# TensorE signals its groups through a drain instead of through the group's last matmul (two-layer kernel, one core)

## The chip, the cores and the metric

One core of one Trainium2 chip runs the kernel. The metric is device microseconds of one execution. TensorE runs matmuls and transpositions, VectorE (DVE), ScalarE (ACT) and GpSimd (POOL) do the element-wise work, SyncE (SP) issues most transfers. All five run their own instruction streams and meet only through semaphores that the kernel writes by hand.

## The reference, cut to what matters

Tokens are x [4, 1024, 128], float32. Two layers, each `x + mixer(norm(x)) + experts(norm(x))`:

```python
xn = layernorm(x)
x  = x + causal_attention(rope(xn @ wq.T), rope(xn @ wk.T), xn @ wv.T)  # scale 1/sqrt(128)
       + top1_experts(xn)         # 8 experts, capacity 512 tokens, one 128x128 matrix each
xn = layernorm(x)
h  = decay * (gelu(gelu(pos @ W1 + b1) @ W2 + b2) @ W3 + b3)            # a filter of 1024 x 128
x  = x + ((xn @ Wu + bu) * fftconv(xn @ Wv + bv, h)) @ Wo + bo
       + top2_experts(xn)         # 8 experts, 128 -> 256 -> relu -> 128
```

## The kernel before, in words

The work is cut into tiles of 128 tokens, 32 in all (`NT`). In order of time TensorE does the following. The order is written out by hand in `@block.tensor` from line 1070 on.

- **Start.** Two filter layers (`filter_layer`). For each of 4 sequences, `transpose_tokens` transposes 8 tiles in two groups of four, and `values_and_gates` multiplies them in four groups of two. Then `routing_counts(0)`.
- **Attention.** 32 rows of 128 queries. Step n of the loop issues `scores(n + 1)`, `transpose_probs(n)` (one or two groups), `weigh_values(n - 1)`. Between them stand `project` (queries and keys of the next sequence), `filter_layer(2)`, `filter_spectrum`, the eight experts of the first layer (`expert0_rows`, `expert0_out`) and `gates` of the second layer.
- **Middle.** `project_vu(0)` to `(3)`, `gates(3)`, `routing_counts(1)`, `project_vu(4)` to `(15)`. GpSimd then scatters 64 times rows to expert slots (line 758), in step with the transforms (`behind_transforms`).
- **Transforms.** `forward` 16 times and `inverse` 12 times, each one `dft` of four products of 128x256.
- **Experts.** The loop over 72 tiles (line 1366). Step n issues `expert_rows(n + 2)` (one transposition), `expert_hidden(n + 1)` (two products) and `expert_out(n)` (two products), plus the four last `inverse`, and `transpose_y` and `project_y` eight times each. ScalarE copies the weights of a tile's expert (line 1032) and the transposed rows (1039); ScalarE and VectorE take the hidden layer by turns (1046, 1748); VectorE adds the bias (1758); GpSimd sends the rows back (767).
- **Tail.** SyncE loads the returned rows, the other engines add them and the result is stored. TensorE has no work there.

All matmuls are issued by the helper `mm`, so the profile puts them on line 1077 whatever function they are from. A float32 product is two MATMUL instructions and two LDWEIGHTS; a transposition is one of each. A group is what stands between two signals. In the kernel before, the group's last instruction carries the signal:

```python
                for f in range(2):
                    last = mm(S[0][:, n % 2, f * P:(f + 1) * P], w12r[:, n % W_RING, f * P:(f + 1) * P], xsT[:, n % 2, :])
                last.then_inc(e_h, 1)
```

Of the kernel before, what the change touches and what calls it, by code (L numbers as in the profile page):

```python
# [26 lines left out]
P = 128  # L27
D = 128
# [3 lines left out]
J = L // P  # L32
# [190 lines left out]
def two_layer_kernel(nc, x_in, cst_in, rope_in, fw_in, iv_in, pe_in, wqk_in, wvg_in, w0_in, b0_in,  # L223
# [3 lines left out]
    with ctx:  # L227
# [847 lines left out]
        def _(pe):  # L1075
# [15 lines left out]
            def values_and_gates(g):  # L1091
                for u in range(4):
                    n = 4 * g + u
                    pe.wait_ge(tr_free, 2 * g + u // 2 + 1)
                    if n >= 2:
                        pe.wait_ge(vg_free, n - 1)
                    for q in range(2):
                        i = 2 * n + q
                        last = mm(O[n % 2][:, q * VGW:(q + 1) * VGW], xT[:, i * P:(i + 1) * P], wvg)
                    last.then_inc(vg_full, 1)  # L1100

            def routing_counts(k):

                pe.wait_ge(rt, (R0_OH, R1_OH)[k])
                if k:
                    pe.wait_ge(lg1_done, B)
                    pe.wait_ge(o_done, NT)
                oh = ohb[:, :, :].rearrange("p e i -> p (e i)")
                mm(O[0][:, 0:E * NT], beforeb[:, :], oh)
                mm(O[0][:, E * NT:2 * E * NT], onesb[:, :], oh).then_inc(rt_mm, 1)  # L1110

            def filter_layer(k):

                if k:
                    pe.wait_ge(f_pool, 4 * k)
                if k < 2:
                    for h in range(2):
                        r = (pe_sb[0:FO, :], hg[0:FO, :])[k][:, 512 * h:512 * h + 512]
                        last = mm(S[k][0:FO, h, :], (f1w, f2w)[k], r)
                else:  # L1120
                    pe.wait_ge(twos_done, 1)
                    for j in range(J):
                        if j % 4 == 0:
                            wait_emptied(pe, T_USES, T_AT[("h", j // 4)])
                        last = mm(t_bank("h", j // 4)[:, (j % 4) * P:(j % 4) * P + P], hg[0:FO + 1, j * P:(j + 1) * P], f3w)
                last.then_inc(f_full, 1)
# [17 lines left out]
            def project(b, h):  # L1144

                for u in (2 * h, 2 * h + 1):
                    n = 4 * b + u
                    slot = S[(n + 1) % 2]
                    wait_scores_bank(("pr", n))
                    for a in range(2):  # L1150
                        last = mm(slot[:, a, :], wqk[:, 2 * (u % 2) + a, :],
                                  xT[:, b * L + 512 * (u // 2):b * L + 512 * (u // 2) + 512])
                    last.then_inc(pr_full, 1)

            def scores(n):
                b, i = n // J, n % J
                wait_scores_bank(("s", n))
                pe.wait_ge(rope_done, 4 * b + (2 if i < 4 else 4))
                q = qk[b % 2][:, 0, i * P:(i + 1) * P]
                for c in range((i + 4) // 4):  # L1160
                    w = min(512, (i + 1) * P - 512 * c)
                    diagonal = c == i // 4
                    last = mm(S[n % 2][:, c, 0:w], q, qk[b % 2][:, 1, 512 * c:512 * c + w], stop=not diagonal)
                    if diagonal:
                        last = mm(S[n % 2][:, c, w - P:w], identb[:, :], maskb[:, :], start=False)
                last.then_inc(s_full, 1)

            def wait_scores_bank(use):

# [5 lines left out]
            def transpose_probs(n):  # L1175
                i = n % J
                pe.wait_ge(exp_done, n + 1)
                for c in range((i + 4) // 4):
                    wait_emptied(pe, T_USES, T_AT[("p", n, c)])
                    for j in range(4 * c, min(4 * c + 4, i + 1)):  # L1180
                        last = pe.transpose(t_bank("p", n, c)[:, (j - 4 * c) * P:(j - 4 * c + 1) * P],  # L1181
                                            prob[n % 2][:, j * P:(j + 1) * P], ident)
                    last.then_inc(pt_full, 1)

            def weigh_values(n):
                b, i = n // J, n % J
                wait_emptied(pe, O_USES, O_AT[("o", n)])
                pe.wait_ge(pt_act, n + 1)
                for j in range(i + 1):
                    if j == 4:  # L1190
                        pe.wait_ge(pt_dve, SECOND.index(n) + 1)
                    last = mm(o_bank("o", n)[:, 0:D], pT[n % 2][:, j, :], vsb[:, b * J + j, :], start=j == 0, stop=j == i)
                last.then_inc(o_full, 1)

            def gates(g):

                for u in (2 * g, 2 * g + 1):
                    wait_emptied(pe, T_USES, T_AT[("t", u)])
                    for q in range(4):
                        pe.wait_ge(xn_done, NT + 4 * u + q + 1)  # L1200
                        last = pe.transpose(t_bank("t", u)[:, q * P:(q + 1) * P], row[:, 4 * u + q, 0:D], ident)
                    last.then_inc(tr_full, 1)
                pe.wait_ge(l1_w_loaded, 16 * N_L1W)
                wait_emptied(pe, O_USES, O_AT[("g", g)])
                for i in range(J * g, J * g + J):
                    pe.wait_ge(tr_free, 2 * B + i // 4 + 1)
                    last = mm(o_bank("g", g)[:, (i % J) * E:(i % J) * E + E], xT[:, i * P:(i + 1) * P], wg1[:, :])
                last.then_inc(g_full, 1)

            def expert0_rows(e):  # L1210
                wait_emptied(pe, T_USES, T_AT[("x", e)])
                for t in range(GROUP):
                    k = GROUP * e + t
                    pe.wait_ge(xs_loaded[k % RING[0]], turn(0, k))
                    last = pe.transpose(t_bank("x", e)[:, t * P:(t + 1) * P], row_slots[0][k % RING[0]][:, 0:D], ident)
                last.then_inc(e_t[0], 1)

            def expert0_out(e):
                pe.wait_ge(moe0_w_loaded, 32)
                pe.wait_ge(e_xT[0], e + 1)  # L1220
                wait_emptied(pe, O_USES, O_AT[("y", e)])
                for t in range(GROUP):
                    last = mm(o_bank("y", e)[:, t * D:(t + 1) * D], xsT0[e % 2][:, t * P:(t + 1) * P], w0[:, e, :])
                last.then_inc(e_y[0], 1)

            pe.wait_ge(filt_loaded, 32)
            filter_layer(0)
# [37 lines left out]
            def project_vu(u):  # L1265
# [4 lines left out]
                for t in range(4):  # L1270
                    i = 4 * (u % 8) + t
                    mm(o[:, t * D:(t + 1) * D], pickb[0:96, :], biasb[0:96, (BV_AT, BU_AT)[u // 8]:(BV_AT, BU_AT)[u // 8] + D],
                       stop=False)
                    last = mm(o[:, t * D:(t + 1) * D], xT[:, i * P:(i + 1) * P], (wv, wu)[u // 8][:, :], start=False)
                last.then_inc(uvg_full, 1)

            pe.wait_ge(exp_done, NT)
            pe.wait_ge(split_done, len(PARTS))
# [41 lines left out]
            def transpose_y(q):  # L1320
# [3 lines left out]
                wait_c_emptied(pe, "yt", q)  # L1324
                for t in range(4):
                    b, j = divmod(4 * q + t, J)
                    last = pe.transpose(c_bank("yt", q)[:, t * P:(t + 1) * P],
                                        vv[b // 2][:, j, (b % 2) * D:(b % 2 + 1) * D], ident)
                last.then_inc(yt_full, 1)

            def project_y(q):
                pe.wait_ge(yt_free, q + 1)
                wait_c_emptied(pe, "wo", q)
                for t in range(4):
                    i = 4 * q + t
                    o = c_bank("wo", q)[:, t * D:(t + 1) * D]
                    mm(o, pickb[0:96, :], biasb[0:96, BO_AT:BO_AT + D], stop=False)
                    last = mm(o, yT[:, i * P:(i + 1) * P], wo[:, :], start=False)
                last.then_inc(wo_full, 1)

            def expert_rows(n):
                pe.wait_ge(xs_loaded[n % RING[1]], turn(1, n))
                if n >= 2:
                    pe.wait_ge(e_xT[1], n - 1)
                pe.transpose(TP[n % 2][:, 0:P], row_slots[1][n % RING[1]][:, 0:D], ident).then_inc(e_t[1], 1)  # L1346

            def expert_hidden(n):
                pe.wait_ge(e_xT[1], n + 1)
# [1 line left out]
                if n >= 2:  # L1351
                    wait_hidden(pe, n - 2)
                for f in range(2):
                    last = mm(S[0][:, n % 2, f * P:(f + 1) * P], w12r[:, n % W_RING, f * P:(f + 1) * P], xsT[:, n % 2, :])
                last.then_inc(e_h, 1)

            def expert_out(n):
                we = w12r[:, n % W_RING, H1 + 2:W_COLS]
# [470 lines left out]
```

## Time and profile before

| | |
|---|---|
| median of 3 runs | 549.97 us (547.23 to 551.78) |
| the profiled execution's own time | 549.17 us |
| its span, first to last instruction | 547.0 us |
| mean granted TensorE clock in the span | 0.864 |
| TensorE busy with matmuls | 385.5 us |
| VectorE, GpSimd, ScalarE busy | 305.4, 284.3, 201.0 us |

In the rows below PE is TensorE's matmuls, PEld its weight loads, and an engine with a q (PEldq) its sequencer. Lines are start, length, engine, line, operation and tiles; the number behind x is a count. In brackets is the time that the engine had stood idle ahead of the instruction and what released it. The ends of matmuls are modelled. A granted clock of 1.00 is 2.4 GHz, 0.50 is 1.2 GHz.

### The profile page before, as it was taken

Reading aid. Unit: us, or ns where it says so; the run is one execution under the profiler, and the core shown is the slowest. Engines: PE = TensorE matmul, PEld = TensorE weight load, DVE = VectorE, ACT = ScalarE, POOL = GpSimd, SP = SyncE. Lnnn points to the kernel's source line nnn. Section 1 sums busy time; section 2 is a strip of 40 time slices with the busy share of each in tenths; the row PEclk is TensorE's granted clock in tenths of the full one; section 3 lists DMA queues with packets and bytes.
Section 4 is the critical chain, followed back from the end, with each engine's and each line's share of the span. In section 5 each row is a group of like instructions: output and inputs, shape, how many; then the busy total and the mean of one; then the engine's idle time right before and its main releaser. Section 6 shows DMA issues by size and latency. Waiting matters only on the chain.

```text
span 547.0 us, 8125 instructions
## 1 busy us (share of the span) xinstructions
PE 385.5 (70%) x2228; PEld 307.3 (56%) x2228; DVE 305.4 (56%) x807; ACT 201.0 (37%) x501; POOL 284.3 (52%) x283
## 2 busy tenths in 40 slices
PE   2573858869696977987785975934977898778600
PEld 0451425756574655686784753823856887667600
DVE  4968428513672675634989961401456576755364
ACT  1471222233241336532230001122766565656360
POOL 2836465425455577401197775762455555555443
PEclk9998787989798999888699695985999799989955
DMA  9999931723211111100001231313122222221094
GB/s 251 402 224 232 178 70 36 198 71 83 60 53 40 58 40 40 38 1 1 5 11 44 71 104 60 104 48 80 43 79 74 70 64 65 74 76 55 11 324 137
DMA packets 63305, 50.27 MB, mean 92 GB/s; under 512 B 7314, under 2 KB 58200, under 8 KB 63006
## 3 DMA queue, kind: packets, MB, share of 16 engines
q1 hardware_dynamic: 56704, 36.92, 27.1%
q0 software_dynamic: 6400, 12.50, 7.2%
q10 hardware_dynamic: 158, 0.33, 0.3%
q8 instruction: 19, 0.31, 0.2%
q14 instruction: 24, 0.20, 0.1%
HBM read 26.18 MB, written 24.22 MB: 92 GB/s over the span
## 4 chain that ended last, share of the span: by engine, by line
PE 24%; POOL 11%; issue 11%; DVE 6%; ACT 3%; DMA 2%; another core or an unknown queue 2%; ACTq 1%; DVEq 1%; POOLq 0%; SPq 0%
PE psS L1077 12%; POOL slots L758 11%; PE psO L1077 9%; PE psT L1346 1%; DVE xres L1780 1%; DMA work<-moe 1%; ACTq L1029 1%; ACT row L958 1%; ACT xsT L1039 1%; DVEq L1754 1%; DVE hT L1748 1%; ACT work L941 0%; DMA slots<-row,slot 0%; ACT xT L964 0%
## 5 line engine op out<-in xcount | busy, mean ns | idle before, releaser
L758 POOL DMA_INDIRECT slots<-row,slot x96 | 109.1, 1136 | 76.1 <-issue 29.0
L767 POOL DMA_INDIRECT moe<-ys,xs x64 | 63.7, 996 | 74.8 <-DVE ys L1758 37.5
L1077 PE MATMUL psS<-work 128*128 128x512 f32 (+3 forms) x96 | 44.0, 574 | 23.2 <-DVE work L1557 13.9
L1077 PE MATMUL psS<-xsT,w12r 128*128 128x128 f32 x288 | 51.5, 306 | 11.7 <-ACT xsT L1039 11.5
L1032 ACT ACTIVATE w12r<-w 128x514 f32 x72 | 45.6, 633 | 30.9 <-PE psO L1077 22.1
L1077 PE MATMUL psO<-w12r,hT 128*128 128x128 f32 x288 | 49.5, 297 | 10.0 <-issue 7.2
L1077 PEld LDWEIGHTS psS<-xsT,w12r 128*128 128x128 f32 x288 | 41.3, 207 | 18.2 <-ACT xsT L1039 15.6
L1077 PEld LDWEIGHTS psO<-w12r,hT 128*128 128x128 f32 x288 | 40.8, 204 | 13.8 <-issue 12.7
L951 ACT ACTIVATE work<-psT 128x512 f32<-128x512 f32 (+3 forms) x32 | 16.5, 515 | 85.2 <-PE psT L1181 72.2
L1077 PE MATMUL psO<-work 128*128 128x128 f32 x288 | 41.6, 294 | 5.3 <-DVE xres L1582 5.3
L1758 DVE TENSOR_TENSOR ys<-psO,b 128x128 f32<-128x128 f32 x72 | 20.8, 289 | 40.8 <-PE psO L1077 29.0
L1748 DVE TENSOR_SCALAR hT<-psS,w12r 128x128 f32<-128x128 f32 x72 | 21.8, 344 | 37.6 <-PE psS L1077 37.0
L1077 PEld LDWEIGHTS psO<-work 128*128 128x128 f32 x288 | 38.6, 210 | 5.5 <-DVE xres L1582 5.5
L1077 PEld LDWEIGHTS psS<-work 128*128 128x128 f32 x96 | 18.7, 224 | 39.8 <-issue 20.4
L1582 DVE SCALAR_TENSOR_TENSOR xres<-psO,work,xres 128x128 f32<-128x128 f32 x32 | 11.1, 348 | 46.3 <-PE psO L1077 28.1
L1077 PE MATMUL psS<-xT,work 128*128 128x512 f32 x64 | 32.5, 649 | 4.5 <-ACT work L941 4.4
L1564 DVE TENSOR_REDUCE work<-psS 128x1 f32<-128x128 f32 (+7 forms) x32 | 24.1, 753 | 20.6 <-PE psS L1077 17.7
L767 POOL DMA_INDIRECT moe<-ys,w x24 | 23.4, 975 | 18.4 <-DVE ys L1758 11.7
L941 ACT ACTIVATE work<-psS,work 128x128 f32<-128x128 f32 (+7 forms) x32 | 23.6, 738 | 17.7 <-DVE work L1568 17.1
L1077 PE MATMUL psS<-xT,mats 128*128 128x256 f32 x96 | 25.6, 410 | 2.3 <-issue 2.2
L1181 PE MATMUL psT<-cst,work 128*128 128x128 f32 x144 | 23.3, 293 | 4.8 <-ACT work L941 4.7
L1017 ACT ACTIVATE work<-psT 128x512 f32<-128x512 f32 x4 | 2.4, 597 | 63.3 <-remote 54.5
(285 smaller groups left out, 863.7 us busy)
## 6 DMA issues: line engine op xcount, KB each, us to landing
slots<-xs SPq DMA_DIRECT2D x13, 516.0 KB, 14.9
xs<-slots SPq DMA_DIRECT2D x64, 64.5 KB
work<-moe SPq DMA_DIRECT2D x8, 512.0 KB, 3.9
xres<-in_x SPq DMA_DIRECT2D x4, 512.0 KB, 9.2
mats<-in_fw SPq DMA_DIRECT2D x1, 2048.0 KB, 11.4
moe<-xs SPq DMA_DIRECT2D x4, 512.0 KB, 7.9
mats<-in_iv SPq DMA_DIRECT2D x8, 256.0 KB
xT<-moe SPq DMA_DIRECT2D x4, 512.0 KB, 8.2
```

The lines of the kernel that those rows point to most:

```text
L758: pool.indirect_dma_start(dst[:, :], bass.IndirectOffsetOnAxis(ap=slots[:, i:i + 1], axis=0), row[:, i, :], None, bounds_check=bound, oob_ ...
L767: pool.indirect_dma_start(dst[:, :], bass.IndirectOffsetOnAxis(ap=row_slots[l][m][:, D:ROWW].bitcast(I32), axis=0), ys[:, n % UNROLL, :], ...
L941: act.activation(prob[n % 2][:, 0:(i + 1) * P], S[n % 2][:, :, :].rearrange("p a m -> p (a m)")[:, 0:(i + 1) * P], ACT.Exp, bias=negmax[:, ...
L951: act.activation(pT[n % 2][:, 0:k, :].rearrange("p j q -> p (j q)"), t_bank("p", n, 0)[:, 0:k * P], ACT.Copy).then_inc(pt_act, 1)
L958: act.activation(row[:, i, 0:D], xres[:, i, :], ACT.Identity, bias=nbias[:, i:i + 1], scale=rstd[:, i:i + 1]).then_inc(xn_done, 1)
L1032: act.activation(w12r[:, n % W_RING, :], w12[:, bass.ds(e, 1), :].rearrange("p e h -> p (e h)"), ACT.Copy).then_inc(e_w1, 1)
L1077: return pe.matmul(o, lhsT, rhs, start=start, stop=stop)
L1181: last = pe.transpose(t_bank("p", n, c)[:, (j - 4 * c) * P:(j - 4 * c + 1) * P], prob[n % 2][:, j * P:(j + 1) * P], ident)
L1564: dve.tensor_reduce(negmax[:, n:n + 1], S[n % 2][:, :, :].rearrange("p a m -> p (a m)")[:, 0:(n % J + 1) * P], X, ALU.max, negate=True).th ...
L1582: stt(xres[:, n, :], o_bank("o", n)[:, 0:D], rrec[:, n:n + 1], xres[:, n, :], ALU.mult, ALU.add).then_inc(o_done, 1)
L1748: last = ts(hT[:, n % 2, f, :], S[0][:, n % 2, f * P:(f + 1) * P], w12r[:, n % W_RING, H1 + f:H1 + f + 1], 0.0, ALU.add, ALU.max)
L1758: tt(ys[:, m, :], O[n % 2][:, 0:D], b2[:, bass.ds(e, 1), :].rearrange("p e d -> p (e d)"), ALU.add).then_inc(e_ys[1], 1)
```

## The change

In every function of `@block.tensor` that signals, the increment no longer rides on the last matmul or transposition of the group. A `pe.drain()` is issued behind it and carries the increment. Matmuls, transpositions, weight loads, waits and the order of the groups stay as they are. In the diff, cut to the forms that it takes:

```diff
@@ transpose_tokens
-                        last = pe.transpose(TP[u][:, q * P:(q + 1) * P], row[:, i, 0:D], ident)
-                    last.then_inc(tr_full, 1)
+                        pe.transpose(TP[u][:, q * P:(q + 1) * P], row[:, i, 0:D], ident)
+                    pe.drain().then_inc(tr_full, 1)
@@ routing_counts
-                mm(O[0][:, E * NT:2 * E * NT], onesb[:, :], oh).then_inc(rt_mm, 1)
+                mm(O[0][:, E * NT:2 * E * NT], onesb[:, :], oh)
+                pe.drain().then_inc(rt_mm, 1)
@@ dft
-                    last = mm(o[n], mats[:, c, 2 * n + 1, :], a[:, 1, :], start=False)
-                last.then_inc(s, 1) if s else None
+                    mm(o[n], mats[:, c, 2 * n + 1, :], a[:, 1, :], start=False)
+                pe.drain().then_inc(s, 1) if s else None
@@ expert_rows
-                pe.transpose(TP[n % 2][:, 0:P], row_slots[1][n % RING[1]][:, 0:D], ident).then_inc(e_t[1], 1)
+                pe.transpose(TP[n % 2][:, 0:P], row_slots[1][n % RING[1]][:, 0:D], ident)
+                pe.drain().then_inc(e_t[1], 1)
@@ expert_out
-                mm(O[n % 2][:, 0:D], hT[:, n % 2, 1, :], we[:, D:2 * D], start=False).then_inc(e_y[1], 1)
+                mm(O[n % 2][:, 0:D], hT[:, n % 2, 1, :], we[:, D:2 * D], start=False)
+                pe.drain().then_inc(e_y[1], 1)
...
```

The same is done in `values_and_gates`, `filter_layer`, `project`, `scores`, `transpose_probs`, `weigh_values`, `gates`, `expert0_rows`, `expert0_out`, `project_vu`, `transpose_y`, `project_y` and `expert_hidden`.

## Rows read from the trace of the kernel before

**Rows 1.** The page, busy time and instructions of each engine.
```profile
PE 385.5 (70%) x2228; PEld 307.3 (56%) x2228; DVE 305.4 (56%) x807; ACT 201.0 (37%) x501; POOL 284.3 (52%) x283
```
**Rows 2.** Busy time in six stretches: start, attention, middle, transforms, experts, tail.
```profile
core 0: us, PE busy (x) PEld busy (x) DVE busy (x) ACT busy (x) POOL busy (x), PEclk, DMA share, GB/s
0.00:53.70 53.70, 25.71 (x114) 16.78 (x114) 39.36 (x123) 20.40 (x51) 28.33 (x25) 0.97 1.09 279
53.70:248.10 194.40, 157.41 (x868) 114.63 (x869) 97.64 (x287) 66.76 (x157) 94.79 (x105) 0.88 0.30 69
248.10:283.80 35.70, 27.36 (x216) 25.64 (x215) 28.23 (x68) 11.29 (x21) 14.16 (x5) 0.85 0.01 3
283.80:376.90 93.10, 59.77 (x224) 47.30 (x224) 44.02 (x86) 7.69 (x13) 64.42 (x65) 0.79 0.23 69
376.90:515.00 138.10, 115.25 (x808) 102.90 (x808) 80.40 (x213) 84.69 (x227) 68.82 (x70) 0.93 0.24 66
515.00:547.00 32.00, 0.00 (x0) 0.00 (x0) 15.73 (x31) 10.20 (x32) 13.79 (x15) 0.55 0.62 197
```
**Rows 3.** TensorE's waits among the experts, 376.9 to 515: total, times, longest.
```profile
PE psS L1077 <- ACT xsT L1039: 11.5, 13, 1.6
PE psO L1077 <- issue: 7.2, 6, 1.9
PE psO L1077 <- DVE hT L1748: 2.5, 5, 0.8
PE psS L1077 <- DVE xres L1741: 1.2, 2, 0.7
```
**Rows 4.** The block's end (line 227), TensorE's sequencer: duration min/median/max.
```profile
L227 PEldq DRAIN  x1: 712/712/712, 514.3 to 514.3; - x1
```
**Rows 5.** Timeline of the last products of TensorE.
```profile
514.29 0.68 PE L1077 MATMUL psO<-w12r,hT 128*128 128x128 f32 x4 [0.21 <-DVE hT L1748]
```
**Rows 6.** One tile each at clock 0.50 and 1.00, TensorE back to back.
```profile
425.58 1.06 PE L1077 MATMUL psS<-xsT,w12r 128*128 128x128 f32 x4
426.44 1.06 PE L1077 MATMUL psO<-w12r,hT 128*128 128x128 f32 x4
427.29 0.42 PE L1346 MATMUL psT<-cst,xs 128*128 128x128 f32 x1
427.50 1.06 PE L1077 MATMUL psS<-xsT,w12r 128*128 128x128 f32 x4
...
429.42 0.61 PE L1077 MATMUL psS<-xsT,w12r 128*128 128x128 f32 x4
429.87 0.61 PE L1077 MATMUL psO<-w12r,hT 128*128 128x128 f32 x4
430.32 0.27 PE L1346 MATMUL psT<-cst,xs 128*128 128x128 f32 x1
430.43 0.68 PE L1077 MATMUL psS<-xsT,w12r 128*128 128x128 f32 x4
```
**Rows 7.** One hidden-layer instruction, 404 to 412 and then 425 to 429: min/median/max ns.
```profile
L1077 PE MATMUL psS<-xsT,w12r x22: 275/275/377, 404.0 to 412.0; 128*128 128x128 f32 x22
```
```profile
L1077 PE MATMUL psS<-xsT,w12r x8: 421/421/421, 425.6 to 428.1; 128*128 128x128 f32 x8
```
**Rows 8.** Waits of TensorE's sequencer in `expert_hidden` (line 1345).
```profile
L1345 PEldq EVENT_SEMAPHORE  x70: 51/51/51, 377.8 to 509.9; - x70
```
**Rows 9.** Timeline of a restart of TensorE behind ScalarE.
```profile
407.05 0.62 ACT L1046 ACTIVATE hT<-psS,w12r 128x128 f32<-128x128 f32 x2 [0.59 <-PE psS L1077]
407.79 0.52 PEld L1077 LDWEIGHTS psO<-w12r,hT 128*128 128x128 f32 x4 [0.75 <-issue]
407.82 0.68 PE L1077 MATMUL psO<-w12r,hT 128*128 128x128 f32 x4 [0.59 <-issue]
```
**Rows 10.** Timeline of TensorE ahead of and in a stretch at clock 0.50 (422.6 to 429.4).
```profile
421.86 0.68 PE L1077 MATMUL psO<-w12r,hT 128*128 128x128 f32 x4 [1.92 <-issue]
422.38 0.27 PE L1346 MATMUL psT<-cst,xs 128*128 128x128 f32 x1
423.50 1.22 PE L1077 MATMUL psS<-xsT,w12r 128*128 128x128 f32 x4 [0.85 <-ACT xsT L1039]
```
**Rows 11.** TensorE's waits in the attention, 53.7 to 248.1.
```profile
PE psS L1077 <- DVE work L1557: 13.9, 5, 5.2
...
PE psO L1077 <- DVE xres L1582: 5.3, 1, 5.3
...
PE psT L1215 <- DMA xs<-slots: 4.0, 1, 4.0
```
**Rows 12.** Timeline where the transforms start and end, and at the first expert tile.
```profile
283.82 2.40 PE L1077 MATMUL psS<-work,mats 128*128 128x256 f32 x10 [1.50 <-DVE work L635]
```
```profile
359.77 1.97 PE L1077 MATMUL psO<-xT,mats 128*128 128x256 f32 x8 [0.89 <-issue]
376.94 0.88 PE L1346 MATMUL psT<-cst,xs 128*128 128x128 f32 x2 [15.20 <-DMA xs<-slots]
```
**Rows 13.** The program's start (line 1820), TensorE's sequencer.
```profile
L1820 PEldq DRAIN  x1: 8/8/8, 0.3 to 0.3; - x1
```

More of the change, by code:

```diff
@@ L1098, in values_and_gates @@
                         i = 2 * n + q
-                        last = mm(O[n % 2][:, q * VGW:(q + 1) * VGW], xT[:, i * P:(i + 1) * P], wvg)
-                    last.then_inc(vg_full, 1)
+                        mm(O[n % 2][:, q * VGW:(q + 1) * VGW], xT[:, i * P:(i + 1) * P], wvg)
+                    pe.drain().then_inc(vg_full, 1)
             def routing_counts(k):
@@ L1118, in filter_layer @@
                         r = (pe_sb[0:FO, :], hg[0:FO, :])[k][:, 512 * h:512 * h + 512]
-                        last = mm(S[k][0:FO, h, :], (f1w, f2w)[k], r)
+                        mm(S[k][0:FO, h, :], (f1w, f2w)[k], r)
                 else:
@@ L1124, in filter_layer @@
                             wait_emptied(pe, T_USES, T_AT[("h", j // 4)])
-                        last = mm(t_bank("h", j // 4)[:, (j % 4) * P:(j % 4) * P + P], hg[0:FO + 1, j * P:(j + 1) * P], f3w)
-                last.then_inc(f_full, 1)
+                        mm(t_bank("h", j // 4)[:, (j % 4) * P:(j % 4) * P + P], hg[0:FO + 1, j * P:(j + 1) * P], f3w)
+                pe.drain().then_inc(f_full, 1)
             def dft(o, a, c, s):
@@ L1150, in project @@
                     for a in range(2):
-                        last = mm(slot[:, a, :], wqk[:, 2 * (u % 2) + a, :],
+                        mm(slot[:, a, :], wqk[:, 2 * (u % 2) + a, :],
                                   xT[:, b * L + 512 * (u // 2):b * L + 512 * (u // 2) + 512])
-                    last.then_inc(pr_full, 1)
+                    pe.drain().then_inc(pr_full, 1)
             def scores(n):
@@ L1162, in scores @@
                     diagonal = c == i // 4
-                    last = mm(S[n % 2][:, c, 0:w], q, qk[b % 2][:, 1, 512 * c:512 * c + w], stop=not diagonal)
+                    mm(S[n % 2][:, c, 0:w], q, qk[b % 2][:, 1, 512 * c:512 * c + w], stop=not diagonal)
                     if diagonal:
-                        last = mm(S[n % 2][:, c, w - P:w], identb[:, :], maskb[:, :], start=False)
-                last.then_inc(s_full, 1)
+                        mm(S[n % 2][:, c, w - P:w], identb[:, :], maskb[:, :], start=False)
+                pe.drain().then_inc(s_full, 1)
             def wait_scores_bank(use):
@@ L1180, in transpose_probs @@
                     for j in range(4 * c, min(4 * c + 4, i + 1)):
-                        last = pe.transpose(t_bank("p", n, c)[:, (j - 4 * c) * P:(j - 4 * c + 1) * P],
+                        pe.transpose(t_bank("p", n, c)[:, (j - 4 * c) * P:(j - 4 * c + 1) * P],
                                             prob[n % 2][:, j * P:(j + 1) * P], ident)
-                    last.then_inc(pt_full, 1)
+                    pe.drain().then_inc(pt_full, 1)
             def weigh_values(n):
@@ L1191, in weigh_values @@
                         pe.wait_ge(pt_dve, SECOND.index(n) + 1)
-                    last = mm(o_bank("o", n)[:, 0:D], pT[n % 2][:, j, :], vsb[:, b * J + j, :], start=j == 0, stop=j == i)
-                last.then_inc(o_full, 1)
+                    mm(o_bank("o", n)[:, 0:D], pT[n % 2][:, j, :], vsb[:, b * J + j, :], start=j == 0, stop=j == i)
+                pe.drain().then_inc(o_full, 1)
             def gates(g):
@@ L1200, in gates @@
                         pe.wait_ge(xn_done, NT + 4 * u + q + 1)
-                        last = pe.transpose(t_bank("t", u)[:, q * P:(q + 1) * P], row[:, 4 * u + q, 0:D], ident)
-                    last.then_inc(tr_full, 1)
+                        pe.transpose(t_bank("t", u)[:, q * P:(q + 1) * P], row[:, 4 * u + q, 0:D], ident)
+                    pe.drain().then_inc(tr_full, 1)
                 pe.wait_ge(l1_w_loaded, 16 * N_L1W)
@@ L1206, in gates @@
                     pe.wait_ge(tr_free, 2 * B + i // 4 + 1)
-                    last = mm(o_bank("g", g)[:, (i % J) * E:(i % J) * E + E], xT[:, i * P:(i + 1) * P], wg1[:, :])
-                last.then_inc(g_full, 1)
+                    mm(o_bank("g", g)[:, (i % J) * E:(i % J) * E + E], xT[:, i * P:(i + 1) * P], wg1[:, :])
+                pe.drain().then_inc(g_full, 1)
             def expert0_rows(e):
@@ L1214, in expert0_rows @@
                     pe.wait_ge(xs_loaded[k % RING[0]], turn(0, k))
-                    last = pe.transpose(t_bank("x", e)[:, t * P:(t + 1) * P], row_slots[0][k % RING[0]][:, 0:D], ident)
-                last.then_inc(e_t[0], 1)
+                    pe.transpose(t_bank("x", e)[:, t * P:(t + 1) * P], row_slots[0][k % RING[0]][:, 0:D], ident)
+                pe.drain().then_inc(e_t[0], 1)
             def expert0_out(e):
@@ L1222, in expert0_out @@
                 for t in range(GROUP):
-                    last = mm(o_bank("y", e)[:, t * D:(t + 1) * D], xsT0[e % 2][:, t * P:(t + 1) * P], w0[:, e, :])
-                last.then_inc(e_y[0], 1)
+                    mm(o_bank("y", e)[:, t * D:(t + 1) * D], xsT0[e % 2][:, t * P:(t + 1) * P], w0[:, e, :])
+                pe.drain().then_inc(e_y[0], 1)
             pe.wait_ge(filt_loaded, 32)
@@ L1273, in project_vu @@
                        stop=False)
-                    last = mm(o[:, t * D:(t + 1) * D], xT[:, i * P:(i + 1) * P], (wv, wu)[u // 8][:, :], start=False)
-                last.then_inc(uvg_full, 1)
+                    mm(o[:, t * D:(t + 1) * D], xT[:, i * P:(i + 1) * P], (wv, wu)[u // 8][:, :], start=False)
+                pe.drain().then_inc(uvg_full, 1)
             pe.wait_ge(exp_done, NT)
@@ L1326, in transpose_y @@
                     b, j = divmod(4 * q + t, J)
-                    last = pe.transpose(c_bank("yt", q)[:, t * P:(t + 1) * P],
+                    pe.transpose(c_bank("yt", q)[:, t * P:(t + 1) * P],
                                         vv[b // 2][:, j, (b % 2) * D:(b % 2 + 1) * D], ident)
-                last.then_inc(yt_full, 1)
+                pe.drain().then_inc(yt_full, 1)
             def project_y(q):
@@ L1337, in project_y @@
                     mm(o, pickb[0:96, :], biasb[0:96, BO_AT:BO_AT + D], stop=False)
-                    last = mm(o, yT[:, i * P:(i + 1) * P], wo[:, :], start=False)
-                last.then_inc(wo_full, 1)
+                    mm(o, yT[:, i * P:(i + 1) * P], wo[:, :], start=False)
+                pe.drain().then_inc(wo_full, 1)
             def expert_rows(n):
@@ L1353, in expert_hidden @@
                 for f in range(2):
-                    last = mm(S[0][:, n % 2, f * P:(f + 1) * P], w12r[:, n % W_RING, f * P:(f + 1) * P], xsT[:, n % 2, :])
-                last.then_inc(e_h, 1)
+                    mm(S[0][:, n % 2, f * P:(f + 1) * P], w12r[:, n % W_RING, f * P:(f + 1) * P], xsT[:, n % 2, :])
+                pe.drain().then_inc(e_h, 1)
             def expert_out(n):
```

## The prediction

> **What bounds the kernel now.** I read the page's busy times first. TensorE leads with 385.5 of 547.0 us [rows 1]. That average hides stages with different limits, so I cut the span into six stretches [rows 2]. Among the experts TensorE is busy 115.3 of 138.1 us, in the attention 157.4 of 194.4, and no other engine reaches 62% of either stretch. Its waits among the experts sum to 22.4 us in 26 pieces, none over 1.9 us [rows 3]. Those two stages, 332 of 547 us, are TensorE's. The other four are not, or only partly. The start is shared with loads and VectorE. In the middle TensorE leads into the routing and VectorE finishes it. The transforms are set by GpSimd: TensorE's last inverse transform starts at 359.8, and its next instruction waits 15.2 us for rows that GpSimd scatters [rows 12]. The tail has no TensorE work.
>
> **How many drains.** One per signal, from the loops.
> - Start: 2 filter layers + 8 transposition groups + 16 value groups + 1 routing = 27.
> - Attention: 16 projections + 32 scores + 48 transposition groups + 32 value products + 1 filter layer + 4 spectra + 8 + 8 experts + 9 in the first three `gates` = 158.
> - Middle: 16 + 3 + 1 = 20.
> - Transforms: 16 forward + 12 inverse = 28.
> - Experts: 3 x 72 + 4 inverse + 8 + 8 = 236.
>
> The sum is 469. No matmul is added or taken away.
>
> **What one drain does.** The old program has a drain on TensorE at its end. It begins at 514.3 and takes 712 ns, so it ends near 515.02 [rows 4]. The four products that it covers start at 514.29 and end at 514.97 [rows 5]. It was issued with three of the four still to start, held its sequencer until all were complete, and ended 0.05 us later. That 0.05 us is what a drain adds to a signal that another engine is waiting for. A start rounded to 0.1 us leaves 0.00 to 0.09.
>
> The larger part is what it takes from TensorE. Now the next group follows the last product at the pace of the stream. One tile takes 430.43 - 429.42 = 1.01 us for nine instructions, 0.11 each [rows 6]. One instruction by itself takes 0.275 from start to end [rows 7]. With a drain the next group can't be issued until the last has ended. From the last start to the next I count four steps:
> - 0.275 to the end of the last product;
> - 0.05 for the drain;
> - 0.05 for the EVENT_SEMAPHORE that most groups have for their further waits [rows 8];
> - 0.06 for LDWEIGHTS and the start of the matmul. ScalarE ends at 407.67 and the matmul starts at 407.82, 0.15 later. Of that 0.05 is the EVENT_SEMAPHORE and about 0.04 the way of the signal [rows 9].
>
> That is 0.435 in place of 0.11, so 0.32 lost. A group that starts on an empty engine takes 0.68 instead of 0.61 [rows 6, 9], 0.07 more. One drain at a place where TensorE ran on therefore costs 0.39 us at clock 1.00. At clock 0.50 the instruction takes 0.421 [rows 7], the pace is (427.50 - 425.58) / 9 = 0.213 [rows 6], and a group after a wait takes 1.22 in place of 1.06 [rows 6, 10]. There a drain costs 0.421 + 0.16 - 0.213 + 0.16 = 0.53. The lowest bound is a drain that adds no gap beyond completion, 0.275 - 0.11 = 0.165. The highest is 0.53 everywhere. I take 0.39 because it is built from restarts that this trace has.
>
> **Experts.** Of 236 places 26 have a wait already [rows 3], and no gap is added there. 210 x 0.39 = 82 us. The new gaps give ScalarE and VectorE time to answer, so the 22.4 us of waits can vanish: 82 - 22 = 60. Without that it is 82. With more overlap than I see, 48.
>
> Then the clock. It was 0.50 from 422.6 to 429.4, just behind waits of 1.92 and 0.85 us, and rose behind a run of tiles back to back [rows 6, 10]. A regular tile now holds 1.01 us of streaming. With three gaps it takes 1.01 + 3 x 0.39 = 2.18, and no regular stretch is back to back any more. So I expect more falls, and fewer of the runs behind which the clock rose. A tile at 0.50 takes 1.92 + 3 x 0.53 = 3.51 us, 1.33 more. I take a third of the tiles, 24 x 1.33 = 32 us, less some 6 that the present low stretches cost already: +26. With two thirds it is 48 x 1.33 - 6 = +58. The dense projections and inverse transforms lie between and should lift it again. Experts: 60 + 26 = 86 us, from 48 to 118.
>
> The Trainium skill (TensorE: Matmul & The Clock Gate, "A second HAM failure mode: psum-queue depth-cycling") describes a kernel whose frequent small idles between groups made the gate swing between its two levels. The trace agrees as far as its falls stand behind waits; it holds no stretch with small gaps alone.
>
> **Attention.** 158 places, some 21 with a wait already: 137 x 0.39 = 53.4. Waits on something not itself behind TensorE can swallow gaps: 5.3 for VectorE's `xres`, 4.0 for a load, and a few of the 13.9 for VectorE's rotations [rows 11]. I take 12. The rotations start with a TensorE signal, so most of that wait stays. Later signals at the waits add 21 x 0.05 = 1, and a few more low stretches 4 (the clock is 0.88 there already [rows 2]). 46 us, from 30 to 62 + 8.
>
> **Start.** 27 places at 0.39 are 10.5. Part of it lies beside loads and VectorE's 39 busy microseconds [rows 2]. 7 us, from 3 to 10.
>
> **Middle and transforms.** `project_vu(0)` to `(3)` and `gates(3)` lead into the routing: 7 x 0.39 = 2.7. The twelve later `project_vu` add 4.7 beside VectorE, while the first transform has 1.5 us of idle ahead of it [rows 12], so 3.2 shows there. Behind it GpSimd's scatters set the pace, with 15.2 us of TensorE idle at the end as cover for the 28 drains (28 x 0.39 = 11). If that cover were gone, all 48 would cost 19. I take 6, from 3 to 15.
>
> **Tail.** Nothing.
>
> **Sum.** 7 + 46 + 6 + 86 = 145 us. The profiled execution took 549.2 (span 547.0 and 2.2 around it), which is 0.8 below the median of the runs, nothing here. 549.2 + 145 = 694.
>
> **Rivals.**
> - *The clock stays up.* The gaps are short, and today's falls stand behind gaps over 0.8 us. Against it: three gaps in each tile take over half of its time. Then 7 + 42 + 6 + 60 = 115, so 664.
> - *The clock stays down among the experts.* If once fallen it finds nothing dense to rise behind, two thirds of the tiles run at 0.50. Experts 118, attention 50, middle and transforms 8, start 7: 183, so 732. Against it: the first tiles and each sequence's projections are dense.
> - *A drain costs only the pipeline's tail.* With 0.165 + 0.05 = 0.21 at some 390 places it is 82, less 34 swallowed: 48 us and 597. Against it: restarts here take longer. The Trainium skill (TensorE: Matmul & The Clock Gate, "Single matmul latency") puts the constant part of a lone product at 398 cycles of 2.4 GHz, 166 ns; by its price alone 469 drains would be an estimated 78 us and the time 627. The 0.165 of rows 6 and 7 agrees with it.
> - *Not slower: the drain doesn't hold what is behind it.* If TensorE's queue takes the next weights and matmuls past a drain, only sequencer time is added, hidden because the sequencer runs ahead, and 0.05 us at some 50 waits: 552. It decides for this if the start-to-start distance across a drain stays near 0.11. For it: the first drain takes 8 ns [rows 13]. Against it: TensorE was empty then; the one with work ahead took 712. By the Trainium skill (PSUM — Partial Sum Buffer, "Engine vs sequencer instructions") a drain waits until the engine is fully idle, which would rule this rival out; the 712 ns agree.
>
> **How the numbers follow.** Forecast 0.42 (694), clock up 0.28 (664), clock down 0.20 (732), tail only 0.07 (597), not slower 0.03 (552). The low end is 3 + 30 + 3 + 48 = 84, so 633. The high end is 10 + 62 + 15 + 118 = 205, so 754. With 0.10 below and some 0.07 above, the range 633 to 755 holds about eight in ten. A change of about 1% can be told from none. Faster by over 1%: 0.01, for the chance that shifted transfers collide less. Within 1%: 0.02. Slower: 0.97.
>
> **What would show it.** 469 more DRAIN rows on TensorE's sequencer, ending about 0.05 us behind the last product. TensorE's matmul count unchanged. Start-to-start across a group's border 0.4 to 0.5 us in place of 0.11. The experts' stretch 220 to 230 us long with a mean clock near 0.8, the attention's near 240, the tail unchanged at 32. The forecast is wrong if the distance stays under 0.3 (the third rival), if the clock among the experts is over 0.93 (the first) or near 0.6 (the second), or if a large part of the added time stands among the transforms, where I give GpSimd the lead.

## The result and the profile after

The changed kernel takes 766.6 us, the median of 4 runs (757.3 to 784.0), and the kernel before 548.6 (546.8 to 551.8). The forecast was 694 us with a range of 633 to 755, so the direction was right and the size was not. The profiled execution took 770.3 us for a span of 768.2 at a mean granted clock of 0.717. The runs of the changed kernel differ by more than is usual (757.3 us at a mean clock of 0.740, 784.0 at 0.701), and the ratio of 1.385, with a 95% interval of 1.370 to 1.400, takes only the two shorter ones, 757.3 and 762.8, as the later ratios leave out the slower executions too and so are not the quotients of the medians beside them.

The page of the changed kernel, busy times, answers to [rows 1]. The second line is the granted clock over 40 slices of the span, in tenths.

```profile
PE 576.0 (75%) x2228; PEld 396.1 (52%) x2228; DVE 310.5 (40%) x807; ACT 208.2 (27%) x501; POOL 285.0 (37%) x283
...
PEclk9997789869979997755899867555555555555555
```

TensorE has the same 2228 matmuls and is "busy" 190 us longer. No other engine gained more than 7.2 us. The trace has 8594 instructions in place of 8125, one more for each of the 469 drains. From slice 26 on the clock is 5 without a break. The six stretches of [rows 2], cut at the same places of the program within 1 us:

```profile
0.00:72.20 72.20, 43.02 (x114) 24.75 (x115) 39.38 (x123) 20.84 (x51) 28.38 (x25) 0.97 1.06 244
72.20:307.20 235.00, 191.64 (x865) 119.69 (x866) 99.24 (x286) 66.91 (x157) 94.25 (x105) 0.87 0.16 46
307.20:362.80 55.60, 43.00 (x219) 35.45 (x219) 28.41 (x69) 11.40 (x21) 27.85 (x19) 0.59 0.06 18
362.80:444.00 81.20, 59.22 (x224) 42.56 (x225) 43.97 (x86) 7.80 (x13) 51.15 (x51) 0.90 0.23 68
444.00:736.80 292.80, 239.09 (x808) 173.69 (x808) 83.79 (x213) 91.09 (x227) 70.26 (x71) 0.53 0.11 31
736.80:768.20 31.40, 0.00 (x0) 0.00 (x0) 15.75 (x31) 10.21 (x32) 13.08 (x14) 0.50 0.63 201
```

| stretch | before | forecast | after | added |
|---|---|---|---|---|
| start | 53.7 | +7 | 72.2 | +18.5 |
| attention | 194.4 | +46 | 235.0 | +40.6 |
| middle and transforms | 128.8 | +6 | 136.8 | +8.0 |
| experts | 138.1 | +86 | 292.8 | +154.7 |
| tail | 32.0 | 0 | 31.4 | -0.6 |

The 0.97 in the start's row is no reading of the clock there. The matmuls of that stretch have the lengths of half clock, as two rows further down show.

The drains among the experts, behind the hidden layer, and a tile of the changed kernel:

```profile
L1357 PEldq DRAIN  x72: 685/1195/1200, 445.3 to 732.7; - x72
```
```profile
561.39 0.45 PE L1347 MATMUL psT<-cst,w 128*128 128x128 f32 x1 [0.23 <-issue]
...
562.06 1.20 PE L1077 MATMUL psS<-xsT,w12r 128*128 128x128 f32 x4 [0.23 <-ACT w12r L1032]
...
563.49 1.19 PE L1077 MATMUL psO<-w12r,hT 128*128 128x128 f32 x4 [0.23 <-issue]
...
564.91 0.45 PE L1347 MATMUL psT<-cst,w 128*128 128x128 f32 x1 [0.23 <-issue]
```

The drain holds the sequencer for the length of its group, here 1.19 us. Behind 226 of the 236 groups of the stretch TensorE stands idle for some 0.23 us, although nothing that the next group needs is late. The tile takes 564.91 - 561.39 = 3.52 us, and 3.51 was forecast for a tile at clock 0.50. TensorE's waits of [rows 3] have gone into these pieces of 0.23:

```profile
PE psO L1077 <- issue: 16.5, 70, 0.3
PE psT L1347 <- issue: 16.3, 70, 0.3
PE psS L1077 <- ACT w12r L1032: 12.1, 52, 0.3
```

### The profile page after: what moved, and what is told of

The parts are those of the page before. It is cut to its first block, busy times and chain, and to the rows that moved or that the text cites. A ratio compares the mean times of both kernels' runs of the same rounds, so it can differ in the third digit from the quotient of the medians.

```text
span 768.2 us, 8594 instructions
## 1 busy us (share of the span) xinstructions
PE 576.0 (75%) x2228; PEld 396.1 (52%) x2228; DVE 310.5 (40%) x807; ACT 208.2 (27%) x501; POOL 285.0 (37%) x283
## 4 chain that ended last, share of the span: by engine, by line
PEld 22%; issue 16%; PEldq 13%; DVE 6%; ACT 5%; DMA 2%; ACTq 0%; POOL 0%; SPq 0%; DVEq 0%; POOLq 0%
PEld psS L1077 14%; PEldq L1366 7%; PEld psO L1077 6%; ACT w12r L1032 4%; PEldq L1357 2%; DVE ys L1711 1%; DVE xres L1783 1%; PEldq L567 1%; DMA work<-moe 1%; PEldq L1134 1%; PEldq L1348 1%; PEld psS L1328 1%; PEld psT L1347 0%; DVE late L1711 0%; DVE hT L1711 0%
## 5 line engine op out<-in xcount | busy, mean ns | idle before, releaser
L1077 PE MATMUL psS<-xsT,w12r 128*128 128x128 f32 x288 | 83.7, 444 | 16.9 <-ACT w12r L1032 12.1
L1077 PE MATMUL psO<-w12r,hT 128*128 128x128 f32 x288 | 83.7, 445 | 16.7 <-issue 16.5
L1077 PEld LDWEIGHTS psS<-xsT,w12r 128*128 128x128 f32 x288 | 65.0, 314 | 35.4 <-issue 34.2
L1077 PEld LDWEIGHTS psO<-w12r,hT 128*128 128x128 f32 x288 | 65.0, 314 | 35.4 <-issue 35.4
L1077 PE MATMUL psO<-work 128*128 128x128 f32 x288 | 45.5, 310 | 10.2 <-issue 8.6
L1077 PE MATMUL psS<-xT,work 128*128 128x512 f32 x64 | 41.0, 775 | 5.0 <-issue 2.8
L1347 PE MATMUL psT<-cst,xs 128*128 128x128 f32 x48 | 20.8, 433 | 20.9 <-issue 10.7
L1182 PE MATMUL psT<-cst,work 128*128 128x128 f32 x144 | 27.9, 307 | 8.9 <-issue 6.6
L1046 ACT ACTIVATE hT<-psS,w12r 128x128 f32<-128x128 f32 x72 | 22.5, 363 | 37.6 <-PEq L1357 37.6
L1077 PE MATMUL psS<-biasb,pickb 96*128 96x128 bf16 x96 | 27.9, 291 | 3.3 <-issue 2.1
```

Of the source, the lines that this page charges most:

```text
L1046: last = act.activation(hT[:, n % 2, f, :], S[0][:, n % 2, f * P:(f + 1) * P], ACT.Relu, bias=w12r[:, n % W_RING, H1 + f:H1 + f + 1])
L1077: return pe.matmul(o, lhsT, rhs, start=start, stop=stop)
```

## The experiments

Most kernels of this section are made with one helper in the place of the 469 drains, and a variable `stage` that names the stretch:

```diff
+            def signal(s):
+                if stage[0] in ("experts",):      # or the stretches that an experiment names
+                    pe.drain().then_inc(s, 1)
+                else:
+                    last[0].then_inc(s, 1)        # the group's last matmul or transposition
-                pe.drain().then_inc(e_h, 1)
+                signal(e_h)
```

**Where the time is: drains by stretch.** The helper as above; the second run has the other four stretches instead.

> Drains only among the experts (236 of 469), elsewhere the signal rides on the last instruction as before. Theory A (the gaps behind the drains thin the stream so that the granted clock falls and does not come back in this stretch): the experts' stretch is 294 us as in the changed kernel, against 138 before, its clock about 0.53, the other stretches as before: 549 + 156 = 705 us. Rival B (the low clock there was chance or was brought along from the stages ahead): the clock among the experts is over 0.85 and the stretch some 200 us, in all about 610 us.

> Drains everywhere but among the experts (233 of 469). Theory A: start +19, attention +41, middle +19, transforms -13 as the two profiles stand against each other, experts 138 us at a clock near 0.93: 549 + 66 = 615 us. Rival B (low clock brought along): the experts' stretch is well over 138 us with a clock under 0.8 though it has no drain.

With drains among the experts alone it took 694.8 us (690.6 to 697.3) where the kernel before took 550.3 on the same chip: +144.5. The other way round it took 614.6 (608.4 to 617.6): +64.3. Together that is 209 of the 218 us by which the medians differ. The experts' stretch of the first, then of the second:

```profile
371.70:657.50 285.80, 232.20 (x808) 168.45 (x808) 83.73 (x213) 90.72 (x227) 70.42 (x71) 0.55 0.11 32
```
```profile
439.60:574.30 134.70, 111.17 (x808) 100.32 (x808) 80.21 (x213) 83.90 (x227) 69.19 (x70) 0.96 0.24 67
```

The low clock comes with the drains of this stretch and isn't brought along: behind stages full of drains, tiles without them run at 0.96. That is theory A.

**Late signal or late start.** All 469 drains stay, but the signal goes back to the last instruction ahead of them. Then, a second drain behind each.

```diff
             def signal(s):
+                last[0].then_inc(s, 1)
-                pe.drain().then_inc(s, 1)
+                pe.drain()
```

> All 469 drains stay, but the signal rides on the last instruction of the group again, ahead of the drain. Theory A (the cost is that TensorE starts its next group late): within 12 us of the changed kernel, 750 to 770 us. Rival D (the cost is that the other engines hear later): most of the added 218 us goes away, 550 to 620 us.

> A second drain behind each of the 469. Theory A: TensorE is empty when it comes, so it costs some 0.05 us of sequencer time, 469 x 0.05 = 23 us: 780 to 795 us. Rival F (a drain has a price of its own of the size of a restart, 0.3 us or more): over 880 us.

The first took 755.9 us (754.5 to 758.4). The other engines hear at once again, and the added time is still there: 205.6 of 218 us by the medians, and all of it by the ratios, 1.388 against 1.385. It is TensorE's own late start that costs. Even what is left is mostly not the earlier signal. The experts' stretch of this trace is 276.2 us where the changed kernel's is 292.8. A tile takes 3.48 us in place of 3.52, which is 3 us in all. The rest comes from the clock, which fell later: between the first inverse transforms and its fall there are 13 plain tiles of some 2.32 us here, and one in the trace of the changed kernel. The second took 806.2 (804.9 and 807.4, two runs only), 40 more than the median with one drain, where 13 to 28 were expected. A row of it shows the piece of idle at 0.30 where it was 0.23:

```profile
605.98 1.19 PE L1080 MATMUL psS<-xsT,w12r 128*128 128x128 f32 x4 [0.30 <-issue]
```

So a drain on an empty engine costs 0.07 us by this row, and 0.08 by the spans of the two profiles (805.3 - 768.2 = 37 us for 469), somewhat more than the 0.05 I gave it, and far from a restart. Rival F falls.

**The two small stretches.** The helper with "start" and with "middle" alone.

> Drains only in the start, 27 of 469. Theory A: in the changed kernel the clock first rose at 64.4 us and not at 26.6, so the start is 18 us longer: first score product at 72 us where it was 54, in all 567 us. Rival H (27 drains at the price of clock 1.00, 0.39 us, no more): 10.5 us, first score product by 64 us, 560 us or less.

> Drains only in the middle, 20 of 469. Theory A: the projections fall to clock 0.50 and stay there, the middle takes 55 us in place of 36; GpSimd starts its scatters at the same time as before, so the transforms give about 10 back: 556 to 562 us. Rival I (VectorE and GpSimd hide all of it): middle at most 42 us and 549 to 552 us in all.

Start alone: 563.7 us (560.6 to 570.1) where the kernel before took 545.9, ratio 1.036 (1.024 to 1.049). The first score product stands at 72.1, as in the changed kernel. 27 drains cost 18 us, 0.67 each, more than the 0.53 of clock 0.50. The rest is the clock, as the value groups show. First the kernel before, two groups in one line, then two late groups of the changed kernel:

```profile
27.63 1.19 PE L1077 MATMUL psO<-work,xT 128*128 128x136 f32 x8 [0.25 <-ACT xT L870]
```
```profile
51.28 1.24 PE L1077 MATMUL psO<-work,xT 128*128 128x136 f32 x4 [0.23 <-issue]
52.75 1.25 PE L1077 MATMUL psO<-work,xT 128*128 128x136 f32 x4 [0.23 <-issue]
```

Eight instructions took 1.19 us, now four take 1.24. Before, these groups ran at full clock from 27 us on. In the changed kernel the last of them, at 52.75, is still at half clock, and so are those of the kernel with drains in the start alone.

Middle alone: 553.6 us (548.8 to 555.7) where the kernel before took 545.9, ratio 1.022 (1.009 to 1.034). That is 8 us by the medians and 12 by the ratio, within the 7 to 13 of theory A (556 to 562 less 549) and over the 0 to 3 of rival I, though the profiled execution, the shortest of its runs, shows only 2 us more in these two stretches. The middle and the transforms of it:

```profile
243.70:297.60 53.90, 42.69 (x221) 35.09 (x218) 28.62 (x69) 11.39 (x21) 26.74 (x18) 0.60 0.05 16
297.60:374.80 77.20, 54.46 (x225) 44.77 (x225) 43.80 (x86) 7.69 (x13) 52.26 (x52) 0.88 0.24 73
```

The middle runs at 0.60 and takes 18 us more than before, and the transforms give 16 of it back. GpSimd's first and last scatter of this run:

```profile
268.06 1.12 POOL L758 DMA_INDIRECT slots<-row,slot  x1 [20.55 <-DVE slot L1709]
...
370.49 0.97 POOL L758 DMA_INDIRECT slots<-row,slot  x1 [0.30 <-issue]
```

They lie 102.4 us apart. In the kernel before it was 101.8 (270.81 to 372.59), in the one with all drains 107.7 (331.86 to 439.55). GpSimd's chain sets the end of the transforms, and the drains of the middle hardly reach it: that is the cover that the forecast gave. The cover isn't whole for the drains of the transforms. Where they are there the chain is 6 us longer, also in the kernel with drains everywhere but among the experts (107.8). In the trace of the changed kernel GpSimd waits 13.5 us in 9 pieces for drains of `dft`.

**One, two, three drains per tile.** The helper asks for the semaphore instead of the stretch.

```diff
-                if stage[0] in ("experts",):
+                if any(s is d for d in (e_h,)):                   # one per tile
+                if any(s is d for d in (e_h, e_y[1])):            # two
+                if any(s is d for d in (e_t[1], e_h, e_y[1])):    # three
```

> Of the drains only the 72 behind the hidden-layer products of the expert tiles. Theory A (the clock stays up while the stream is thick enough, so the cost is not in proportion to the drains): 72 x 0.39 = 28 us less what the 22 us of waits take in, clock among the experts over 0.85: 555 to 575 us. Rival E (each drain costs its share of what all 236 cost there, 145 us): 145 x 72 / 236 = 44, so 594 us.

> Of the drains only the 144 behind the two groups of products of the expert tiles, none behind their transpositions. A tile at clock 1.00 is then 1.01 + 2 x 0.39 = 1.79 us, at 0.50 1.92 + 2 x 0.53 = 2.98. Theory A: the stream is between that of one and of three drains; the clock falls for part of the stretch, 0.7 to 0.95, stretch 172 to 215 us, in all 585 to 625 us. Rival E (in proportion): 145 x 144 / 236 = 88, so 638 us.

> Drains behind all three groups of the 72 expert tiles (216) and nowhere else, so none on the 20 inverse transforms, transpositions and projections of the same stretch. Theory A (the third drain of a tile is what takes the clock): clock under 0.7 among the experts, 670 to 695 us. Rival L (the 20 others are what takes it, by thinning the only dense work there): clock over 0.85 and 590 to 610 us, in line with 568 for one drain per tile and 577 for two.

| drains among the experts | us | before beside it | added | per drain | clock there | stretch |
|---|---|---|---|---|---|---|
| 72 | 567.5 (564.5 to 573.6) | 551.0 | 16.6 | 0.23 | 0.91 | 156.0 |
| 144 | 576.7 (574.9 to 579.7) | 551.0 | 25.8 | 0.18 | 0.97 | 164.4 |
| 216 | 682.9 (681.7 to 689.0) | 548.3 | 134.6 | 0.62 | 0.56 | 272.7 |
| 236 | 694.8 (690.6 to 697.3) | 550.3 | 144.5 | 0.61 | 0.55 | 285.8 |

The stretch of 144 drains, then of 216, then one tile of the first:

```profile
379.70:544.10 164.40, 132.47 (x808) 106.20 (x808) 82.61 (x213) 87.07 (x227) 70.27 (x70) 0.97 0.19 55
```
```profile
375.80:648.50 272.70, 223.56 (x808) 165.12 (x808) 83.73 (x213) 90.72 (x227) 70.36 (x71) 0.56 0.12 33
```
```profile
481.65 0.68 PE L1080 MATMUL psO<-w12r,hT 128*128 128x128 f32 x4 [0.23 <-issue]
...
483.60 0.68 PE L1080 MATMUL psO<-w12r,hT 128*128 128x128 f32 x4 [0.23 <-issue]
```

The first 144 drains are cheap: the waits that were there take in a part of each, and the clock stays up. With 144 it is 0.97, where the kernel before has 0.93. A tile takes 483.60 - 481.65 = 1.95 us. The 1.01 of [rows 6] holds only where nothing waited: from 391.1 to 440.2 the kernel before took 49.0 us for 28 tiles, 1.75 each. The 72 behind one transposition each bring 109 us with them, 1.5 us per drain, and take the clock. The 20 on the denser groups are 10 us. Rival L falls, and so does any account in proportion. Whether it is the number of gaps in a tile that takes the clock, or the transposition that now stands alone between two of them, isn't tested: no run has two drains of which one is behind the transposition. For two drains my own expectation (585 to 625) was too high, because I looked for falls of the clock that did not come.

**More work, less time.** One bf16 product of 256 or 384 columns ahead of each of the 216 groups, into columns of the group's own bank that nobody reads. No other engine waits for it.

```diff
+            def filler(o):
+                for r in range(1):                 # 2 in the second of these kernels
+                    mm(o, onesb[0:96, :], biasb[0:96, 0:o.shape[1]])
 ...
+                filler(TP[n % 2][:, P:P + 384])
                 transpose(TP[n % 2][:, 0:P], row_slots[1][n % RING[1]][:, 0:D], ident)
```

> As the kernel with drains only among the experts, and ahead of each of the 216 groups of the tiles one more bf16 product of 256 or 384 columns into unused columns of the group's own bank; its result is used by nobody. Theory A: the stream is thicker, the clock there goes to over 0.85, a tile takes about 2.7 us in place of 3.52 although it has more to do: stretch about 225 us, in all about 636 us, 70 us less than without the filler. Rival C (a drain lowers the clock itself, or the clock has nothing to do with how thin the stream is): the clock stays at 0.5, a tile takes about 4.4 us, in all about 770 us.

> Drains only among the experts, and two fillers ahead of each group instead of one. Theory A: the clock was up with one already, so the second only adds its stream, 0.11 to 0.16 us each at 2.4 GHz: 216 x 0.14 = 30 us, 660 us. Rival K (more stream still gains clock): 630 us or less.

> The changed kernel with all 469 drains and the fillers ahead of the 216 groups of the expert tiles. Theory A: the experts come down from 294 to about 220 us as they did with drains there alone, the other stretches stay: 766 - 70 = 696 us, between 685 and 705. Rival J (with low clock brought along from the stages ahead the fillers don't lift it): 760 us or more.

With drains among the experts alone, one filler per group brings 694.8 us down to 630.3 (626.9 to 634.3). The fillers add 216 matmuls and take 64 us away. The expert stretch:

```profile
377.60:597.80 220.20, 166.10 (x1024) 117.37 (x1022) 83.63 (x213) 90.51 (x227) 70.09 (x70) 0.98 0.15 41
```

The clock is 0.98 in place of 0.55, with every drain still there. So a drain doesn't lower the clock by itself. With two fillers the clock is 0.98 too, the stretch is 252.0 and the run 664.5 (659.2 to 665.2). That is 34 more, the stream of the second filler and nothing gained. In the kernel with all 469 drains one filler gives 699.7 us (692.9 to 703.7), 67 less than the 766.6 of the changed kernel, with 220.6 us for the stretch, the other stretches as they were.

So the drains have two costs, and the clock is the larger. The 64 us that the fillers gave back are less than the clock costs, for the fillers need time themselves. At clock 1.00 a tile with three drains takes 2.35 us (rows in the next section), with one filler per group 2.61 (420.05 to 422.66 in that trace). So one set of fillers is an estimated 72 x 0.26 = 19 us, and the stretch with all its drains, at full clock and without fillers, an estimated 220 - 19 = 201 us. That is 63 over the 138 of the kernel before, for the gaps. The other 92, up to the 293 of the changed kernel, are the clock. The tiles alone say nearly the same: 72 x (3.52 - 2.35) = 84 us. The fillers differ from the other matmuls in more than being additional (bf16, 256 or 384 columns), and which of that brings the clock back isn't shown.

**The same on the kernel before.** No drain; useless products only where TensorE waited anyway.

```diff
             project(0, 0)
+            for _ in range(8):
+                mm(TP[0][:, :], ident, cst[:, 0:512])
 ...
             pe.wait_ge(b_free, INV_BEFORE)
+            for _ in range(12):
+                mm(TP[0][:, :], ident, cst[:, 0:512])
```

> The kernel before with no drain; TensorE gets 8 useless float32 products of 512 columns between its first projection and its wait for the routing, and 12 behind the last inverse transform ahead of the experts, where it waited 8.6 and 15.2 us. Theory A (the clock is up where the stream was thick just before): the low stretches that follow, 50.5 to 60.8 and 376.9 to 381.5, run at 1.00, 3 + 2 us less: 543 to 547 us where the kernel before takes 549 to 550. Rival G (the fillers make what waits late by more than they give): over 552 us.

550.6 us (12 runs) against 551.0 of the kernel before beside it, where 543 to 547 were expected. The ratio is 0.994 (0.991 to 0.998), but the medians are only 0.4 us apart and 4 of the 12 runs take 554 us or more, so a gain of 3 us isn't shown. The clock did come up at both places: it is 1.00 from 50 to 62 us, where the first attention rows of the kernel before (53.7 to 62) have 0.57, and 1.00 from 379 to 384, where its first tiles (376.9 to 381.5) have 0.50. The mean clock among the experts is 0.93 all the same, as before. The attention stretch is 188.9 us, but in the kernel with drains only among the experts, which has neither drains nor fillers there, it is 189.9.

## Why the prediction was wrong in size

- *What bounds the kernel* held. The two stretches that were TensorE's took 195 of the added 221 us of the span, the tail none.
- *The step that failed* is the clock among the experts, "I take a third of the tiles": +26 us in the sum, and an estimated 92 measured. The rest of that stretch came out as forecast, 60 us for the gaps against an estimated 63. The start missed by 11.5 us for the same reason.
- *What a drain does* held in kind. It holds the sequencer until all is complete, and the gap is TensorE's. The page of the Trainium skill by which a drain waits until the engine is idle (PSUM — Partial Sum Buffer, "Engine vs sequencer instructions") is borne out by 72 drains of 1195 ns (median) on groups of 1.19 us.
- *The price of one drain* held at clock 0.50: (3.52 - 1.92) / 3 = 0.53, as forecast. At 1.00 the term of 0.39 was small. A tile in the one stretch at full clock takes 460.67 - 458.32 = 2.35 us in place of 2.18, so 0.45:

```profile
458.32 0.30 PE L1347 MATMUL psT<-cst,xs 128*128 128x128 f32 x1 [0.23 <-issue]
458.85 0.68 PE L1077 MATMUL psS<-xsT,w12r 128*128 128x128 f32 x4 [0.23 <-issue]
459.76 0.68 PE L1077 MATMUL psO<-w12r,hT 128*128 128x128 f32 x4 [0.23 <-issue]
460.67 1.53 PE L1077 MATMUL psS<-xT,mats 128*128 128x256 f32 x6 [0.23 <-issue]
```

  The idle piece is 0.23 and not the 0.16 that I built from a restart. What the other 0.07 are isn't shown. The estimate from the other page of the Trainium skill (TensorE: Matmul & The Clock Gate, "Single matmul latency"), 166 ns per drain, agrees with the pipeline's end (0.275 - 0.11 = 0.165), and holds no more than that: the whole is 0.45 to 0.53, so its 627 us was far too low here.
- *Attention* held in size, +41 for +46, but partly by luck. Its clock stayed at 0.87. TensorE's waits for other engines and loads, without the first one for VectorE, fell from 36.0 to 7.9 us there, so 28 us of gaps were swallowed and not 12. The wait for the rotations, of which I said that most stays, went from 13.9 to 1.4. The gaps must then have cost some 69 us, which is 0.50 for each of my 137 places and not 0.39. The two errors cancel. No run has drains in the attention alone.
- *Middle and transforms* held in size, +8 for +6, and the mechanism in part. GpSimd's scatters did set the pace. But the middle took 20 us more, at clock 0.59, and the transforms 12 less; I had foreseen neither. The first scatter starts 2 us later against the start of the middle (24.7 us in place of 22.7), not the 6 that I gave the drains of the middle. The chain of scatters is 6 us longer, where I gave the drains of the transforms nothing.
- *Experts* failed at "I take a third of the tiles". From 480 us to the end not one tile was at full clock:

```profile
480.00:560.00 80.00, 63.94 (x204) 45.95 (x204) 26.58 (x69) 26.72 (x68) 23.09 (x23) 0.50 0.13 36
560.00:640.00 80.00, 66.08 (x226) 48.52 (x226) 23.28 (x58) 23.70 (x58) 17.75 (x19) 0.50 0.10 30
640.00:736.00 96.00, 78.91 (x268) 57.93 (x268) 25.70 (x65) 27.57 (x68) 22.47 (x23) 0.50 0.08 23
```

  The 67 tiles at 3.52 are 236 us. The other 57 are five tiles between 453 and 473 us, wholly or partly at full clock, and the twenty denser groups. My own sum with all 72 tiles at the lower level adds 60 + 72 x 1.33 - 6 = 150 us to the stretch, and 155 were measured. The rival that had it right, "the clock stays down", got 0.20 and still only two thirds of the tiles. I had counted on the dense groups to lift the clock. In the changed kernel, where they have a drain each as well, the eight transpositions and projections did not. Where they have none (216 drains) those of the first half did, to 1.00 from 510 to 520 us. It fell again in the third tile behind the last of them, and those of the second half did not lift it:

```profile
410.00:500.00 90.00, 72.11 (x231) 52.17 (x232) 30.25 (x77) 29.41 (x76) 26.42 (x26) 0.50 0.13 37
525.00:648.00 123.00, 101.70 (x345) 75.80 (x346) 35.33 (x91) 37.92 (x94) 31.14 (x31) 0.50 0.09 27
```

  So it is the tile with three gaps that doesn't keep the upper level. In the traces with 469, 236 and 216 drains and in the one with the signal ahead of the drain, the clock fell after 1 to 13 such tiles in a row. The price of both levels was in the trace of before; which tile keeps the upper one was not, since it has no stretch with small gaps alone.
- *Start* failed for the same reason. I priced its 27 drains at clock 1.00 (10.5, cut to 7). The clock had risen at 27 us only behind groups of products back to back, and these are the groups that the drains part. It took 18 us.
- The section of the Trainium skill that I cited for the clock (TensorE: Matmul & The Clock Gate, "A second HAM failure mode: psum-queue depth-cycling") describes a swing between the levels. The trace of the changed kernel doesn't agree for the experts: from 480 us on they stay at the lower level for 257 us. In the attention the mean clock is 0.87 with drains and 0.88 without, so no more of a swing shows there either.
- The high end of the range was added up with 62 for the attention, though its own range went to 62 + 8. With the 8 it is 762.

## What to carry to other kernels

Let the signal ride on the matmul: a drain costs TensorE 0.45 to 0.53 us of its own time wherever it would have run on, and the other engines gain nothing by it. When a change puts small gaps into a stream, price the tile at both levels of the clock for all of the stretch, and give the lower level a chance of its own. Which level a tile keeps had to be measured here: at 1.95 us with two gaps it kept the upper one, at 2.35 with three it did not, and at 2.61 with three gaps and fillers it did. The cost of gaps can be a step and not a slope, as 144 drains for 26 us and 72 more for 109 show.

## What was not expected of the hardware

- 216 useless matmuls made a kernel 64 us faster (694.8 to 630.3), with the clock at 0.98 in place of 0.55.
- TensorE can be busy 82% of a stretch by the profile (239.1 of 292.8 us) and be granted 0.53. One instruction counts as 0.275 us busy where the next follows after 0.11 [rows 6, 7], so behind each gap the busy share holds a pipeline's end that a running stream hides.
- The piece of idle behind a drain is 0.23 us at either clock. That suggests that it is the sequencer's and not the array's, but the ends from which it is counted are modelled.
